# A recurrent layer on one Trainium2 core: three planes and a reduce in place of an interleaved scan, and GpSimd in place of a transfer

## The chip, the cores and the metric

The kernel runs on one core of a Trainium2 chip. The core has TensorE (PE) for matmuls, VectorE (DVE), ScalarE (ACT), GpSimd (POOL) and SyncE (SP, transfers), each with its own queue of instructions; they meet only at semaphores. The metric is the device time of the whole program in microseconds. Lower is better. A measurement of this kernel can tell apart about 0.2%, some 17 us.

## The reference

The program computes two layers of a model on x [16, 128, 128] (N = 16 rows, T = 128 steps, D = 128 channels). Each layer has a recurrent or conditioning part, a state space or attention part, a gated recurrence and a feed-forward part. Only the first of these parts is touched, a plain recurrence:

```
xw = einsum('ntd,dh->nth', x, Wx) + b
def step(prev_h, xw_t):
    next_h = tanh(prev_h @ Wh + xw_t)
    return (next_h, next_h)
_, hs = lax.scan(step, h0, swapaxes(xw, 0, 1))
```

The weights are scaled so that the recurrence magnifies small differences. The kernel therefore forms each dot product as the reference's arithmetic does: 128 products, each added in order to a running sum and rounded after each, with the product itself not rounded before the addition.

## The kernel before

The work of this layer is in the function `rnn`. A dot product over k = 0..127 is built in four moves, for all 16 n at once, with the output channels on the 128 partitions.

1. TensorE forms all 16 x 128 products in PSUM, from three bf16 pieces of each operand, with a diagonal matrix as the moving operand (`product`, `h_product`).
2. ScalarE copies them to `pd`; VectorE forms the running sums `s`: a scan for the odd ones (`prefix_odd`, L560, two halves of the n), an addition for the even ones (`prefix_even`, L564).
3. The rounding errors of the running sums are found exactly. VectorE forms the difference s - pd for the hidden half (`difference`, L567, into `gain`). TensorE adds, in PSUM, minus the sums, the difference and the products once more (`remainder`, L295, L300, L303); what is left is the remainder of every step of the sum.
4. A chain adds, for each k, minus the difference, the remainder and the sum to one running number. For this ScalarE writes the three into an interleaved layout `at` (`put_sums`, `put_differences`, `put_remainders`, L391, L394, L397, L400), and VectorE runs a scan that takes two numbers per element (`chain`, L571, four quarters of the n).

All this is done twice. The hidden half (R, prev_h @ Wh) lies on the recurrence. The input half (X, x_t @ Wx) does not depend on h and runs AHEAD = 9 steps in front: nine rounds of a prologue, and then one round beside each of the 128 steps. Its difference comes another way: ScalarE makes a negated copy `nd` of the products (`copy_negative`, L385), and a transfer from the queue of GpSimd adds the sums to it (L477, `accum_op=ALU.add`), with a small instruction ahead of it (L476).

A step runs as follows. VectorE makes h by a rational function (`tanh`, L155 to L238) and cuts it into three bf16 pieces (`pieces`). TensorE makes the hidden product (L278), ScalarE copies it in two halves (L431), and VectorE makes odd and even prefix sums and the difference. While TensorE makes the remainders (L300, L303), a correction for rounding ties (`sticky`, L311, on signs from L436 and L442) and ScalarE puts them (L400), VectorE does the input half: half of the odd scans, the even sums, four chains and their sum with the bias (`xwt`, L589). Then come four hidden chains, `pre` (L621) and tanh. In `tanh`, ScalarE makes three copies (L453 to L455) that the scan L203 waits for.

The queue of TensorE is written out by hand. After the sticky matmuls come the input half's minus sums (L295), differences (L300) and products (L303), then the next input product (L270), then a wait until ScalarE has put the input remainders (`e.wait_ge(xa, 5 * g + 5)`), then 28 filler matmuls (`stay_warm`, L327), in seven lots that wait for places in tanh (`IN_TANH`; the last lot of three waits for h), and then the hidden product of the next step. In every eighth step (s = 7) a transpose (L330) stands before the fillers; in two of eight steps GpSimd also copies stationary operands (L499, L503).

Of the kernel before, what the change touches and what calls it, by code (L numbers as in the profile page):

```python
# [28 lines left out]
BF16 = mybir.dt.bfloat16  # L29
N = 16  # L30
# [5 lines left out]
TANH_SMALL = 0.0004  # L36
# [14 lines left out]
LX = 1 + 3 * NP  # L51


def rnn(nc, ident, hs, w):
    with ExitStack() as ctx:
# [15 lines left out]
        def side(tag):  # L71
            f = dict(pd=sb(tag + "pd", [128, N, K2]), s=sb(tag + "s", [128, N, K2]), d=sb(tag + "d", [128, 2, N * LX + 1]))
            f["at"] = f["d"][:, :, 1:].rearrange("p c (n l) -> p n c l", l=LX)
            return f
        R, X = side("rh_"), side("rx_")
        R.update(part=sb("rh_part", [128, 3, N, 2], BF16), rest=sb("rh_rest", [128, 2, N]),
                 diag=sb("rh_diag", [128, 3, N, KB], BF16), gain=sb("rh_gain", [128, N, D]),
                 sg=sb("rh_sg", [128, 2, NB, 512], BF16))
        X["nd"] = sb("rx_nd", [128, N, K2])
        co = sb("co", [128, N * LX])  # L80
        ends = co[:].rearrange("p (n l) -> p n l", l=LX)[:, :, LX - 1]
        xt = co[:, 0:T * N]
# [3 lines left out]
        pre = sb("pre", [128, N]); cl = sb("cl", [128, N]); x2 = sb("x2", [128, N]); ab = sb("neg", [128, N])  # L86
        mask = sb("mask", [128, N]); big = sb("big", [128, N]); small = sb("small", [128, N])
# [4 lines left out]
        spare = R["gain"][:].rearrange("p n k -> p (n k)")  # L92
# [5 lines left out]
        rc = sb("rc", [128, N]); nn = sb("nn", [128, N]); qq = sb("qq", [128, N]); rcb = sb("rcb", [128, N])  # L98
        hi = sb("hi", [128, N]); lw = sb("lw", [128, N]); dsp = sb("dsp", [128, 2, N]); qsel = sb("qsel", [128, N])
# [5 lines left out]
        xp_mm, xl_mm, xa, xs, xd, xc, xn, xg = (sem(x) for x in ("xp_mm", "xl_mm", "xa", "xs", "xd", "xc", "xn", "xg"))  # L105
# [3 lines left out]
        A_COPIED, A_ODD, A_SEEDED, A_SIGNED, A_PUT = 2, 3, 5, 6, 8  # L109
        KA = A_PUT + 2 * NRC + 1  # L110
        V_ODD, V_EVEN, V_DIFF = 2, 3, 4
        VSUM = V_DIFF + NRC + 1
        VGUESS = VSUM + 8
        KV = VSUM + 44
# [3 lines left out]
        VSETUP = 60  # L118
# [34 lines left out]
        def tanh(tl, e, dep, tripled):  # L153
            tl.wait(dep)
            i = tl.inc(e.tensor_scalar(cl[:], pre[:], -TANH_CLAMP, TANH_CLAMP, ALU.max, ALU.min))  # L155
            n_ = tl.inc(e.tensor_scalar(ab[:], pre[:], -1.0, None, ALU.mult))
            tl.wait(i)
            i = tl.inc(e.tensor_tensor(x2[:], cl[:], cl[:], ALU.mult))
            tl.wait(n_)
# [3 lines left out]
            tl.wait(j)  # L163
            tl.inc(e.tensor_scalar(big[:], mask[:], TANH_SMALL, None, ALU.is_ge))
            tl.inc(e.scalar_tensor_tensor(out=small[:], in0=mask[:], scalar=TANH_SMALL, in1=cl[:], op0=ALU.is_lt, op1=ALU.mult))
# [43 lines left out]
            b_ = tl.inc(e.reciprocal(rc[:], den))  # L209
            a_ = tl.inc(e.tensor_tensor(nn[:], cl[:], num, ALU.mult))  # L210
            i = tl.inc(e.tensor_tensor(raw(dsp[:, 0, :]), raw(den), cut[:, 0:N], ALU.bitwise_and))
            tl.wait(a_)
            q_ = tl.inc(e.tensor_tensor(qq[:], nn[:], rc[:], ALU.mult))
# [3 lines left out]
            i = tl.inc(e.tensor_tensor(raw(hi[:]), raw(qq[:]), cut[:, 0:N], ALU.bitwise_and))  # L217
            p_ = tl.inc(e.tensor_tensor(tq[:, :, 0], qq[:], den, ALU.mult))
            tl.inc(e.tensor_tensor(rcb[:], rc[:], big[:], ALU.mult))
            tl.wait(i)  # L220
            f_ = tl.inc(e.tensor_tensor(lw[:], qq[:], hi[:], ALU.subtract))
# [5 lines left out]
            i = tl.inc(e.tensor_tensor(qsel[:], qq[:], big[:], ALU.mult))  # L227
# [3 lines left out]
            tl.wait(i)  # L231
            tl.inc(e.tensor_tensor(qsel[:], qsel[:], small[:], ALU.add))
            tl.wait(s_)
            r_ = tl.inc(e.tensor_tensor(rm[:], rm[:], tn2[:, :, 4], ALU.subtract))
            tl.wait(r_)
            r_ = tl.inc(e.tensor_tensor(rr[:], rm[:], rcb[:], ALU.mult))
            tl.wait(r_)
            return tl.inc(e.tensor_tensor(h[:], qsel[:], rr[:], ALU.add))  # L238

        def remainder_slots(F, n, odd):  # L240
            dst = F["at"][:, n, 0, 3::3] if odd else F["at"][:, n, 1, 0:LX - 1:3]
            return dst.rearrange("p n (b k) -> p n b k", b=NB)

        def remainder_sums(bank0, n, odd):
            return ps[:, bank0:bank0 + NB, :].rearrange("p b (n k c) -> p n b k c", n=N, c=2)[:, n, :, :, odd]
# [13 lines left out]
        IN_TANH = ((9, 4), (14, 4), (19, 4), (23, 4), (26, 5), (36, 4), (44, 3))  # L259
# [6 lines left out]
        def _(e):  # L266
# [25 lines left out]
            def remainder(bank0, F, stat, mov, prefixed, differenced, diff, last, own=NB, seeded=None):  # L292
                e.wait_ge(*prefixed)
                for b in range(own):
                    e.matmul(ps[:, bank0 + b, :], negid[:], piece(F, "s", b), start=True, stop=False)  # L295
                e.wait_ge(*differenced)
                for b in range(NB):
                    if b == own:
                        e.wait_ge(*seeded)
                    e.matmul(ps[:, bank0 + b, :], ident[:], diff(b), start=False, stop=False, skip_group_check=(b >= own))  # L300
# [47 lines left out]
            with e.Fori(0, T // UN // TURNS) as turn:  # L348
                for i, s in ((TURNS * turn + r, s) for r in range(TURNS) for s in range(UN)):
# [13 lines left out]
                    if s == UN - 1:  # L363
                        e.wait_ge(stl, i + 3)
                    remainder(0, X, xl_stat, x_mov((s + 1) % UN), (xs, 3 * g + 3), (xd, 16 * (g + 1)), x_diff, True).then_inc(xl_mm, 1)
                    if s == UN - 2:
                        e.wait_ge(stp, i + 3)
# [11 lines left out]
        def _(e):  # L379
# [35 lines left out]
            for g in range(AHEAD):  # L415
                if g:
                    e.wait_ge(xc, KXC * g)
# [1330 lines left out]
```

## Time and profile before

| what | value |
|---|---|
| median of 3 runs | 8299.39 us (8298.24 to 8300.0) |
| span of the profiled execution | 8311.2 us |
| recurrent layer, first h to last h | 319.0 to 4998.9 us |
| PE busy | 6754.2 us (81%) |
| DVE busy | 6987.2 us (84%) |
| ACT busy | 4891.1 us (59%) |
| POOL busy | 1902.8 us (23%) |

The profile is of one execution. Its time is its span; no other time of the same execution is at hand. A row of a timeline gives the start and the duration in us, the engine, the line, the operation and its tiles, the number of instructions merged (xN), and in brackets the idle time of the engine before it with what ended it. Shares of busy time are averages over stages with different limits; the order of starts within one step says more.

### The profile page before, as it was taken

To read this page: it belongs to the slowest core of one execution; us is meant where nothing else is said; L and a number is where in the kernel's file an instruction comes from. 1 tells how busy PE (TensorE), PEld (TensorE's weight loads), DVE (VectorE), ACT (ScalarE), POOL (GpSimd) and SP (SyncE) were. 2 spreads that over 40 slices of the span, in tenths; PEclk is the share of its full clock that TensorE was granted. 3 is DMA by queue.
4 is the path that set the end of the run, shared out by engine and by line. 5 is a ranking of instruction groups with operands and counts; after the bars stand their busy time and mean duration, and the time that the engine had idled before them with its cause. 6 is when DMAs were issued, how large, how long until landed. Compare 5 with 4: busy or idle time off the path is not lost. (4 is left out here: it accounts for less than half of the span.)

```text
span 8311.2 us, 122846 instructions
## 1 busy us (share of the span) xinstructions
PE 6754.2 (81%) x38193; PEld 2748.6 (33%) x38193; DVE 6987.2 (84%) x12707; ACT 4891.1 (59%) x5846; POOL 1902.8 (23%) x1514
## 2 busy tenths in 40 slices
PE   4788888888888888888888883588888888782889
PEld 1233333333333333333333331233333333341553
DVE  4799999999999999999999996899999999446333
ACT  3677777777777777777777772244444444222322
POOL 0000001001001001001000110588788888000000
PEclk8999999999999999999999996799999999996999
DMA  1211111111111111111111110000000000000000
GB/s 37 37 27 32 32 27 32 32 27 32 27 32 32 27 32 30 29 32 28 31 32 27 32 32 24 18 4 3 4 3 3 4 3 3 2 6 3 3 15 5
DMA packets 51335, 174.59 MB, mean 21 GB/s; under 512 B 5857, under 2 KB 13794, under 8 KB 49698
## 3 DMA queue, kind: packets, MB, share of 16 engines
q0 software_dynamic: 37264, 145.91, 9.9%
q1 hardware_dynamic: 13586, 22.47, 1.0%
q8 instruction: 273, 4.47, 0.2%
q14 instruction: 212, 1.74, 0.1%
HBM read 15.12 MB, written 7.34 MB: 3 GB/s over the span
## 5 line engine op out<-in xcount | busy, mean ns | idle before, releaser
L980 POOL TENSOR_TENSOR hc<-hh,cg 128x512 f32<-128x512 f32 x1024 | 1290.4, 1267 | 349.8 <-DVE hh L962 349.5
L902 ACT ACTIVATE ps_m<-ps_m,aneg 128x508 f32<-128x508 f32 x1024 | 674.4, 659 | 1121.2 <-DVE hh L962 1011.2
L962 DVE TENSOR_TENSOR_SCAN hh<-ps_m,bx 128x512 f32<-128x512 f32 x1024 | 1228.7, 1213 | 13.7 <-POOL bx L984 13.7
L476 POOL TENSOR_TENSOR r_gate<-ident 128x1 f32<-128x1 f32 x137 | 213.7, 1560 | 4475.4 <-DVE rx_s L564 4413.3
L327 PE MATMUL r_ps<-wdiag,whq 128*128 128x512 bf16 x4480 | 1057.7, 382 | 216.3 <-DVE rh_gain L189 76.4
L866 PE MATMUL ps_m<-hc,pick 128*128 128x512 f32 x2048 | 1056.9, 600 | 8.0 <-POOL hc L980 6.8
L571 DVE TENSOR_TENSOR_SCAN co<-rx_d 128x772 f32<-128x772 f32 x544 | 924.0, 1761 | 0.0
L571 DVE TENSOR_TENSOR_SCAN co<-rh_d 128x772 f32<-128x772 f32 x512 | 862.5, 1747 | 15.6
L300 PE MATMUL r_ps<-rx_nd,ident 128*128 128x512 f32 x1096 | 557.4, 655 | 200.7 <-DMA rx_nd<-rx_s 200.7
L327 PEld LDWEIGHTS r_ps<-wdiag,whq 128*128 128x128 bf16 x4480 | 395.3, 98 | 836.9 <-issue 139.3
L941 DVE TENSOR_TENSOR bx<-ps_m,bg 128x512 f32<-128x512 f32 x896 | 596.8, 672 | 89.4 <-PE ps_m L882 89.0
L877 PE MATMUL ps_m<-rows,ones 128*128 128x512 bf16 x1024 | 403.2, 394 | 266.0 <-ACT ps_m L902 261.7
L400 ACT ACTIVATE rx_d<-r_ps 128x1024 f32<-128x1024 f32 x274 | 406.4, 1568 | 306.1 <-PE r_ps L303 306.1
L394 ACT ACTIVATE rh_d<-rh_s 128x1024 f32<-128x1024 f32 x256 | 419.7, 1639 | 195.3 <-DVE rh_s L560 195.3
L300 PE MATMUL r_ps<-rh_gain,ident 128*128 128x512 f32 x1024 | 473.7, 605 | 42.5 <-DVE rh_gain L567 42.3
L295 PE MATMUL r_ps<-rx_s,negid 128*128 128x512 f32 x1096 | 498.4, 597 | 3.0 <-POOL xsl L503 3.0
L560 DVE TENSOR_TENSOR_SCAN rx_s<-rx_pd 128x520 f32<-128x520 f32 x274 | 337.3, 1234 | 179.2 <-ACT rx_pd L381 151.7
L391 ACT ACTIVATE rx_d<-rx_s 128x2048 f32<-128x2048 f32 x137 | 412.4, 3010 | 72.5 <-DVE xwt L589 70.6
L431 ACT ACTIVATE rh_pd<-r_ps 128x1024 f32<-128x1024 f32 x256 | 248.2, 1022 | 341.9 <-PE r_ps L278 341.9
L400 ACT ACTIVATE rh_d<-r_ps 128x256 f32<-128x256 f32 x1024 | 380.7, 519 | 100.2 <-PE r_ps L311 100.2
L866 PEld LDWEIGHTS ps_m<-hc,pick 128*128 128x128 f32 x2048 | 391.8, 192 | 131.2 <-POOL hc L980 27.9
L877 PEld LDWEIGHTS ps_m<-rows,ones 128*128 128x128 bf16 x1024 | 98.4, 96 | 1008.3 <-ACT ps_m L902 993.1
(412 smaller groups left out, 11921.0 us busy)
## 6 DMA issues: line engine op xcount, KB each, us to landing
rx_nd<-rx_s POOLq DMA_DIRECT2D x137, 1040.0 KB, 8.0
rows_scratch<-pc SPq DMA_DIRECT2D x48, 128.0 KB
rows<-rows_scratch SPq DMA_DIRECT2D x128, 48.0 KB
ew<-in_e SPq DMA_DIRECT2D x3, 1024.0 KB, 7.4
co<-in_x_dn SPq DMA_DIRECT2D x1, 1024.0 KB, 4.8
xcur<-in_x_dn SPq DMA_DIRECT2D x1, 1024.0 KB
out_x<-xcur SPq DMA_DIRECT2D x1, 1024.0 KB, 3.9
qi<-in_f_q SPq DMA_DIRECT2D x1, 384.0 KB, 3.0
```

What stands on the lines that cost most here:

```text
L295: e.matmul(ps[:, bank0 + b, :], negid[:], piece(F, "s", b), start=True, stop=False)
L300: e.matmul(ps[:, bank0 + b, :], ident[:], diff(b), start=False, stop=False, skip_group_check=(b >= own))
L327: e.matmul(ps[:, bank, :], whq[:, 0, :], wdiag[:, 0, 0:N, :].rearrange("p m k -> p (m k)"), start=True, stop=True)
L394: e.activation(F["at"][:, :, c, 2::3], F["s"][:, :, 2 + c:K2:2], ACT.Copy).then_inc(done, 1)
L400: e.activation(remainder_slots(F, n, odd), remainder_sums(bank0, n, odd), ACT.Copy).then_inc(done, 1)
L571: return e.tensor_tensor_scan(co[:, at], F["d"][:, 0, 1:][:, at], F["d"][:, 1, 0:N * LX][:, at], 0.0, ALU.add, ALU.add)
L866: e.matmul(ps[:, 6, :], pick[:, 128 - un:256 - un], hc[un % NHC][:], start=False, stop=True, skip_group_check=True).then_inc(summed, 1)
L877: e.matmul(ps[:, un % 2, :], ones3[:], rows[0][b][:, j, :], start=True, stop=True).then_inc(dt_bc, 1)
L902: e.activation(da[un % NDA][:, :, 1:T], ps[:, un % 2, :].rearrange("p (n t) -> p n t", n=NG4)[:, :, 1:T], ACT.Exp, scale=aneg[:, 0:1]).the ...
L941: e.tensor_tensor(bx[un % NBUF][:], ps[:, 2 + un % 2, :], bg[:], ALU.mult).then_inc(driven, 1)
L962: e.tensor_tensor_scan(hh[un % NBUF][:], da[un % NDA].rearrange("p n t -> p (n t)"), bx[un % NBUF][:], 0.0, ALU.mult, ALU.add).then_inc(sc ...
L980: e.tensor_tensor(hc[un % NHC][:], hh[un % NBUF][:], cg[:], ALU.mult).then_inc(weighted, 1)
```

## The change

The interleaved layout goes. Each half gets three planes, `planes` [128, 3, N, K2], holding minus the difference (pd - s), the remainder and the sum; `s`, `nd` and `rho` are views of them. The chain becomes a `tensor_reduce` over k and, inside it, the plane, for a quarter of the n, so ScalarE only copies remainders (one put per quarter for the hidden half, two for the input half) and no longer copies sums and differences. The input half's even prefix sums and difference are made by GpSimd; the transfer and the negated copy go. In TensorE's queue the input half's minus sums are followed by the next input product, and only then by the differences and products of the remainder. On VectorE the first quarter of the input chain moves ahead of the hidden prefix sums, the other three ahead of both odd scans of the input half. In tanh, the masks and the arithmetic select are replaced by one comparison of the square and a predicated copy. The diff, cut to its core:

```diff
+            f = dict(pd=sb(tag + "pd", [128, N, K2]), planes=sb(tag + "planes", [128, 3, N, K2]), ends=sb(tag + "ends", [128, N]))
+            f["nd"], f["rho"], f["s"] = (f["planes"][:, c] for c in (MINUS_D, RHO, SUM))
...
 def tanh
-            n_ = tl.inc(e.tensor_scalar(ab[:], pre[:], -1.0, None, ALU.mult))
-            j = tl.inc(e.tensor_tensor(mask[:], ab[:], pre[:], ALU.max))
-            tl.inc(e.tensor_scalar(big[:], mask[:], TANH_SMALL, None, ALU.is_ge))
-            tl.inc(e.scalar_tensor_tensor(out=small[:], in0=mask[:], scalar=TANH_SMALL, in1=cl[:], op0=ALU.is_lt, op1=ALU.mult))
+            tl.inc(e.tensor_scalar(small[:], x2[:], TANH_SMALL_SQUARED, None, ALU.is_lt))
...
-            tl.inc(e.tensor_tensor(rcb[:], rc[:], big[:], ALU.mult))
-            i = tl.inc(e.tensor_tensor(qsel[:], qq[:], big[:], ALU.mult))
-            tl.inc(e.tensor_tensor(qsel[:], qsel[:], small[:], ALU.add))
+            tl.inc(e.copy_predicated(quot[:], raw(small[:]).unsqueeze(1).to_broadcast([128, 2, N]), plain[:]))
+            tl.wait(s_ + 1)
...
-        IN_TANH = ((9, 4), (14, 4), (19, 4), (23, 4), (26, 5), (36, 4), (44, 3))
+        IN_TANH = ((6, 4), (11, 4), (16, 4), (20, 4), (23, 5), (32, 4), (39, 3))
...
 tensor, in each step
                     sticky(4, (ra, KA * t + A_SIGNED))
+                    minus_sums(0, X, (xs, 3 * g + 3))
+                    if s == UN - 2:
+                        e.wait_ge(stp, i + 3)
+                    e.wait_ge(ra, KA * t + A_SIGNED + NRC)
+                    product(4, xp_stat, x_mov((s + 2) % UN)).then_inc(xp_mm, 1)
                     if s == UN - 1:
                         e.wait_ge(stl, i + 3)
-                    remainder(0, X, xl_stat, x_mov((s + 1) % UN), (xs, 3 * g + 3), (xd, 16 * (g + 1)), x_diff, True).then_inc(xl_mm, 1)
-                    e.wait_ge(ra, KA * t + A_PUT + 2 * NRC)
-                    product(4, xp_stat, x_mov((s + 2) % UN)).then_inc(xp_mm, 1)
-                    e.wait_ge(xa, 5 * g + 5)
+                    remainder(0, X, xl_stat, x_mov((s + 1) % UN), (xd, g + 1), True).then_inc(xl_mm, 1)
+                    e.wait_ge(xa, KXA * g + 3)
...
 scalar, in each step
-                    put_sums_of(R, 1, ra)
-                    put_sums_of(R, 0, ra)
-                    put_differences(R, R["gain"][:], ra)
                     for c in range(NRC):
-                        for odd in range(2):
-                            put_remainders(R, 4, quarter(c), odd, ra)
-                    e.wait_ge(xc, KXC * g)
-                    parts(g, 0)
+                        put_remainders(R, 4, quarter(c), ra)
                     (the three copies t1, t1, t0)
+                    x_remainders(g)
+                    x_products(g + 1)
-                    copy_out(X, 4, xa)
-                    copy_negative(xn)
...
 gpsimd
             def x_difference(g):
+                e.wait_ge(xc, KXC * g)
+                e.wait_ge(xs, 3 * g + 2)
+                e.tensor_tensor(X["s"][:, :, 2:K2:2], X["s"][:, :, 1:D:2], X["pd"][:, :, 2:K2:2], ALU.add).then_inc(xs, 1)
                 e.wait_ge(xs, 3 * g + 3)
-                e.tensor_tensor(gate[:, 2:3], ident[:, 0:1], ident[:, 1:2], ALU.add).then_inc(xg, 1)
-                e.dma_start(flat(X["nd"][:]), flat(X["s"][:]), accum_op=ALU.add, max_dma_last_dim=4 * N * K2 // 2).then_inc(xd, 16)
+                e.tensor_tensor(X["nd"][:, :, 2:K2], X["pd"][:, :, 2:K2], X["s"][:, :, 2:K2], ALU.subtract).then_inc(xd, 1)
...
 vector
+            def chain(F, n):
+                return e.tensor_reduce(F["ends"][:, n], F["planes"][:, :, n, 2:K2].rearrange("p c n k -> p n k c"), XY, ALU.add)
...
-                    x_prefix_odd(g, HALVES[0])
+                    x_chain_first(g - 1)
                     (hidden odd and even prefix sums, difference)
-                    x_prefix_odd(g, HALVES[1])
-                    x_prefix_even(g)
-                    x_chain(g - 1, s)
+                    x_chain_rest(g - 1, s)
+                    x_prefix(g)
                     (four hidden chains, pre, tanh, pieces)
```

## Rows read from the trace of the kernel before

**Rows 1.** The line that writes h: starts over all steps; duration min/median/max in ns.

```profile
L238 DVE TENSOR_TENSOR h<-qsel,rr x128: 174/174/178, 319.0 to 4998.9; 128x16 f32<-128x16 f32 x128
```

**Rows 2.** Timeline of VectorE in one ordinary step.

```profile
2417.01 0.17 DVE L238 TENSOR_TENSOR h<-qsel,rr 128x16 f32<-128x16 f32 x1
...
2420.72 2.37 DVE L560 TENSOR_TENSOR_SCAN rh_s<-rh_pd 128x520 f32<-128x520 f32 x2 [0.41 <-ACT rh_pd L431]
...
2426.60 1.24 DVE L560 TENSOR_TENSOR_SCAN rx_s<-rx_pd 128x520 f32<-128x520 f32 x1
...
2429.01 6.73 DVE L571 TENSOR_TENSOR_SCAN co<-rx_d 128x772 f32<-128x772 f32 x4
...
2436.08 6.74 DVE L571 TENSOR_TENSOR_SCAN co<-rh_d 128x772 f32<-128x772 f32 x4
2442.85 0.18 DVE L621 TENSOR_TENSOR pre<-co,xwT 128x16 f32<-128x16 f32 x1
...
2453.13 0.18 DVE L238 TENSOR_TENSOR h<-qsel,rr 128x16 f32<-128x16 f32 x1
```

**Rows 3.** Timeline of TensorE in the same step.

```profile
2432.42 1.90 PE L311 MATMUL r_ps<-rh_sg,r_tau 128*128 128x512 bf16 x8
2434.16 3.60 PE L295 MATMUL r_ps<-rx_s,negid 128*128 128x512 f32 x8
2438.74 3.70 PE L300 MATMUL r_ps<-rx_nd,ident 128*128 128x512 f32 x8 [0.98 <-DMA rx_nd<-rx_s]
2442.38 2.12 PE L303 MATMUL r_ps<-wdiag,xsl 32*128 32x512 bf16 x36
2444.33 1.46 PE L270 MATMUL r_ps<-wdiag,xsp 32*128 32x512 bf16 x24
2447.65 6.54 PE L327 MATMUL r_ps<-wdiag,whq 128*128 128x512 bf16 x28 [1.85 <-DVE rh_gain L189]
2454.14 1.60 PE L278 MATMUL r_ps<-rh_diag,whq 32*128 32x512 bf16 x24
```

**Rows 4.** Timeline of ScalarE in the same step.

```profile
2419.66 1.94 ACT L431 ACTIVATE rh_pd<-r_ps 128x1024 f32<-128x1024 f32 x2 [2.14 <-PE r_ps L278]
...
2434.36 2.97 ACT L400 ACTIVATE rh_d<-r_ps 128x256 f32<-128x256 f32 x8 [0.80 <-PE r_ps L311]
...
2444.55 2.97 ACT L400 ACTIVATE rx_d<-r_ps 128x1024 f32<-128x1024 f32 x2 [1.52 <-PE r_ps L303]
```

**Rows 5.** VectorE's groups by line and form: busy us, mean ns, idle before.

```profile
L138 DVE TENSOR_TENSOR rh_part<-rh_rest,nought 128x32 bf16<-128x32 f32 x258 | 47.6, 184 | 0.0
...
L225 DVE TENSOR_TENSOR tq<-lw,dsp 128x32 f32<-128x32 f32 x128 | 25.1, 196 | 0.0
...
L1340 DVE TENSOR_REDUCE fmu<-fyc 128x16 f32<-128x2048 f32 x3 | 6.9, 2286 | 0.1
...
L1516 DVE TENSOR_REDUCE amu<-aoa 128x256 f32<-128x2048 f32 x1 | 3.6, 3566 | 0.0
...
L1495 DVE TENSOR_REDUCE aaq<-ae 128x256 f32<-128x1024 f32 x1 | 1.2, 1220 | 0.0
```

**Rows 6.** Two lines of GpSimd: duration min/median/max in ns.

```profile
L980 POOL TENSOR_TENSOR hc<-hh,cg x1024: 1260/1266/1447, 5272.8 to 7064.9; 128x512 f32<-128x512 f32 x171
...
L476 POOL TENSOR_TENSOR r_gate<-ident x137: 193/1572/1582, 49.5 to 4974.9; 128x1 f32<-128x1 f32 x137
```

**Rows 7.** Timeline of TensorE in a step whose transfer landed late.

```profile
2549.21 5.40 PE L300 MATMUL r_ps<-rx_nd,ident 128*128 128x512 f32 x8 [2.35 <-DMA rx_nd<-rx_s]
...
2559.78 6.21 PE L327 MATMUL r_ps<-wdiag,whq 128*128 128x512 bf16 x28 [1.83 <-ACT rx_d L400]
```

**Rows 8.** Windows: busy time of each engine, granted clock (PEclk), DMA share, GB/s.

```profile
2549.00:2552.00 3.00, 2.79 (x4) 1.26 (x5) 2.97 (x3) 3.00 (x2) 0.00 (x0) 0.58 0.00 0
```

**Rows 9.** VectorE's waits between 400 and 4900 us: total us, times, longest.

```profile
DVE rh_s L560 <- ACT rh_pd L431: 86.8, 122, 2.5
DVE to L203 <- ACT t L455: 36.4, 24, 2.0
```

More of the change, by code:

```diff
@@ L50 @@
 TURNS = 2
-LX = 1 + 3 * NP
+MINUS_D, RHO, SUM = 0, 1, 2
+XY = mybir.AxisListType.XY
 def rnn(nc, ident, hs, w):
@@ L290, in residue, with minus_sums @@
                 return ins
-            def remainder(bank0, F, stat, mov, prefixed, differenced, diff, last, own=NB, seeded=None):
+            def minus_sums(bank0, F, prefixed, own=NB):
                 e.wait_ge(*prefixed)
@@ L295, in remainder @@
                     e.matmul(ps[:, bank0 + b, :], negid[:], piece(F, "s", b), start=True, stop=False)
+            def remainder(bank0, F, stat, mov, differenced, last, own=NB, seeded=None):
                 e.wait_ge(*differenced)
@@ L564, in prefix_even @@
                 return e.tensor_tensor(F["s"][:, :, 2:K2:2], F["s"][:, :, 1:D:2], F["pd"][:, :, 2:K2:2], ALU.add)
-            def difference(out, F):
-                return e.tensor_tensor(out, F["s"][:, :, 2:K2], F["pd"][:, :, 2:K2], ALU.subtract)
-            def chain(F, lo, hi_):
-                at = slice(lo * LX, hi_ * LX)
-                return e.tensor_tensor_scan(co[:, at], F["d"][:, 0, 1:][:, at], F["d"][:, 1, 0:N * LX][:, at], 0.0, ALU.add, ALU.add)
-            def x_prefix_odd(g, part, later=True):
-                e.wait_ge(xa, 5 * g + 1)
-                if later:
-                    e.wait_ge(xd, 16 * g)
-                prefix_odd(X, part).then_inc(xs, 1)
@@ new lines, in chain, with x_prefix, x_chain_first, x_chain_rest @@
+            def chain(F, n):
+                return e.tensor_reduce(F["ends"][:, n], F["planes"][:, :, n, 2:K2].rearrange("p c n k -> p n k c"), XY, ALU.add)
+            def x_prefix(g):
+                e.wait_ge(xa, KXA * g + 1)
+                for part in HALVES:
+                    prefix_odd(X, part).then_inc(xs, 1)
+            def x_chain_first(g):
+                e.wait_ge(xa, KXA * g + 2)
+                chain(X, quarter(0)).then_inc(xc, 1)
+            def x_chain_rest(g, u):
+                tx = Tally(e, xc, KXC * g + 1)
+                e.wait_ge(xa, KXA * g + 3)
+                for c in range(1, NXC):
+                    tx.inc(chain(X, quarter(c)))
@@ L588, in x_chain @@
                 tx.wait(tx.n)
-                tx.inc(e.tensor_tensor(xwt[:, N * u:N * (u + 1)], ends, brow[:, N * u:N * (u + 1)], ALU.add))
+                tx.inc(e.tensor_tensor(xwt[:, N * u:N * (u + 1)], X["ends"][:], brow[:, N * u:N * (u + 1)], ALU.add))
             for g in range(AHEAD):
-                for part in HALVES:
-                    x_prefix_odd(g, part, g > 0)
-                x_prefix_even(g)
                 if g:
-                    x_chain(g - 1, g - 1)
+                    x_chain_first(g - 1)
+                    x_chain_rest(g - 1, g - 1)
@@ L609, in _ @@
                     tl.wait(j)
[L610 to L614 removed]
+                    tl.inc(difference(R))
+                    x_chain_rest(g - 1, s)
+                    x_prefix(g)
                     for c in range(NRC):
[L616 to L617 removed]
+                        e.wait_ge(ra, KA * t + A_SIGNED + c + 1)
+                        j = tl.inc(chain(R, quarter(c)))
                     tl.wait(j)
@@ L620, in _ @@
                         e.wait_ge(xw_cp, i + 1)
-                    j = tl.inc(e.tensor_tensor(pre[:], ends, xwT[:, s, :], ALU.add))
+                    j = tl.inc(e.tensor_tensor(pre[:], R["ends"][:], xwT[:, s, :], ALU.add))
                     j = tanh(tl, e, j, (tri, 3 * t + 3))
```

160 lines of the change are left out of this document (53 added, 107 removed).

## The prediction

> **What bounds the kernel now.** I read the page first: VectorE and TensorE are both busy for over four fifths of the span, so shares alone do not say which decides. Then the 128 steps of the recurrent layer, by the starts of the instruction that writes h: 319.0 to 4998.9 us over 127 steps, 36.85 us each [rows 1]. The change touches nothing behind them. The timelines of one ordinary step say what sets its length [rows 2 to 4]. The reader is to see a ring. VectorE's rows stand nearly back to back from the hidden half's prefix sums (2420.72) to h (2453.13); the only hole is 0.41 us before the prefix sums, waiting for ScalarE's copy of the new product. TensorE runs the input half's work from 2434.16 to 2445.79, with a hole of 0.98 us for the transfer, waits for ScalarE's puts, and starts the 28 filler matmuls at 2447.65. They end at 2454.19, and the next hidden product starts at 2454.14. The last three fillers wait for h, so VectorE decides, but TensorE arrives only just in time. I count all times below from D = 2426.60, the start of VectorE's first row behind the hidden difference. In these terms: hidden chains start at 9.48, `pre` at 16.25, fillers at 21.05, next hidden product 27.54 to 29.14.
>
> **The prices first.** *Reduce.* A quarter goes from a scan over 772 pairs (four take 6.74, thus 1.66 from start to start [rows 2]) to a reduce over 4x128x3 = 1536 numbers. Reduces over 2048 and 1024 contiguous numbers take 2286 and 1220 ns, so 1.04 ns a number and 154 fixed; one over 2048 whose inner step is 64 bytes takes 3566 ns, 1.67 a number [rows 5]. Then 1536 numbers cost 1.75 us at full rate and 2.71 us at the strided rate; 0.08 less from start to start. The new reduce takes each number from another plane, 8320 bytes off, and returns to the first plane's neighbour after three. No row shows that pattern. The nearest in form is L225: its second input alternates between two rows 64 bytes apart and takes 196 ns for 32 elements, against 184 for L138 and some 20 ns more that the strided rate would add [rows 5]; so an alternation of two lines seems free, a round of eight (L1516) is not, and three lies between. I take the full rate, and keep the strided one as a rival.
>
> The Trainium skill speaks against this step. "Advanced Engine Details and Errata", section Memory Cachelines, says that accesses which each hit another 16-byte line are penalised; by it every reduce would pay the strided rate. "Vector Engine (DVE) Microarchitecture Reference", section Measured stream behaviour on trn2, gives 1.73 ns for a source that hops with every element, but full rate for one stream alternating between two regions. The rows above bear out both, and neither page has three planes. By the first rule the time would be that of rival B below, 9010 us; by the second, carried over to three planes, my sum.
>
> *GpSimd.* A two-input operation over 512 numbers takes 1260 ns at least, and one over a single number 193 ns when alone [rows 6]: 2.09 ns a number. The even prefix sums (1024) are then 2.33 us and the difference (2048) 4.47 us. Bounds for the first: 1.23, what VectorE takes for it, and 2.52, twice the row. The row with 1572 ns for one number stands beside a VectorE scan with two inputs in SBUF: the engines can block each other. In the new order VectorE runs reduces (one input) while GpSimd works, and GpSimd's 1260 ns row holds beside VectorE work with only one SBUF input; I take no blocking.
>
> *ScalarE.* It loses the copies of sums and differences into the interleaved layout and the negated copy. That is worth only what waits for it: VectorE's wait before L203, 36.4 us in all [rows 9]. A put of a quarter is now one row of 512 numbers, about 0.6 us, between the old puts of 256 (eight in 2.97) and copies of 1024 (two in 1.94) [rows 4].
>
> *Tanh.* Seven small rows go, two come. They mostly filled gaps that a dependency leaves anyway (cl to x2 to xm start 0.21 apart with or without them). The predicated copy has no row; between 0.11 and 0.25 us as other small ones, and the subtraction now waits for it. Net -0.05, bounds -0.3 and +0.2.
>
> **A step of the new kernel, from D.** VectorE: three input chains 5.07 us, the sum into xwt and two odd prefix scans (1.15 + 1.23) end at 7.6. The hidden chains wait for the first put: the sticky matmuls end at 7.72 as before, ScalarE puts 0.6, start 8.4 in place of 9.48. Four chains bring `pre` to 15.15, 1.1 earlier, and h to 25.4. The input chain moved before the hidden prefix sums takes 1.66 where a scan of 1.23 with 0.41 of waiting stood: nothing lost beyond 0.1.
>
> TensorE is now late instead. Its first input matmuls need the even prefix sums, which VectorE had ready long before and GpSimd delivers at 7.65 + 2.33, so they start at 10.05 in place of 7.56. Everything queued behind them in order follows: eight f32 matmuls with the sums 3.64 (as from 2438.74 to 2442.38 [rows 3]), the next input product 1.30 (24 of the 36 from 2442.38 to 2444.33), the difference matmuls 3.64 and the 36 remainder matmuls, 2.17 to ScalarE's start: 20.8. GpSimd's difference is done by 14.6, under the product, and costs nothing. ScalarE's two puts are one pair of 1024 from PSUM, 1.94 [rows 4]: 22.75. The fillers wait for these puts and start at 22.9 in place of 21.05, although h now comes earlier. Twenty-eight of them cannot be skipped: in the step of 2559.78, where they did not wait for h, they still took 6.2 us [rows 7]. The hidden product so starts at 29.05 and, all its inputs ready, takes 1.46 as the input product of the same size: it ends at 30.5 in place of 29.14. From there ScalarE's copy, the prefix sums and the difference follow as before. **Plus 1.4 us a step**; VectorE's gain of 1.1 turns into waiting for the hidden product.
>
> Two corrections. In 30 of the 125 steps between 330 and 4990 us the transfer into rx_nd lands late and TensorE stands 2.2 to 2.4 us (the row of 2549.21 is one); I take each as 0.9 us longer, since an ordinary step takes 36.12 (h at 2417.01 and 2453.13 [rows 2]) and the mean is 36.85, of which the loop's own turns leave about a third to them. With no transfer that ends: -27 us. But in 18 of these 30 TensorE then ran its f32 matmuls at a lower granted clock (0.58 over 2549 to 2552, 5.40 us in place of 3.70 [rows 7, 8]); after the 95 shorter gaps never. The new order makes a gap of 2.3 us (7.72 to 10.05) in every step. With 18 in 30: 0.6 x 1.7 = 1.0 us, now on the path: +131 us. The prologue (nine rounds without the hidden half, before 319.0) swaps the 8 us transfer for GpSimd's 6.9 and loses two memsets, but puts a chain before each prefix scan; nothing, within 30. GpSimd's copies for xsp and xsl now stand ahead of its two operations, but fall in the previous tanh, where VectorE has slack. Sum: 128 x 1.4 = 179, -27, +131 = **+283 us**, on 8299.39: **8582 us**, say 8580. The profiled execution spans 8311.2, 12 us over the median of the runs; I carry that over.
>
> **The rivals.** *B, the reduce pays the strided rate* (for it: L1516; against it: L225). Input chains end at 7.97, prefix scans at 10.5, hidden chains take 10.6: `pre` at 21.1, 4.85 later, and the chain moved ahead delays the prefix sums by 2.63 - 1.64 = 1.0. TensorE then has slack, bar the clock. 5.85 x 128 = 749, less some 40 for the late steps: about 9010, up to 9080 with the low clock.
>
> *F, TensorE keeps up* (the other side). If fillers end before h, VectorE's sum holds: -1.1 + 0.1 - 0.05 = -1.05 a step, 134 us, and the waits for ScalarE beyond the usual 0.41, (86.8 - 122 x 0.41) + 36.4 = 73 us [rows 9]: 8092. It decides only where the input puts are done by `pre` + 4.9; my sum has them at `pre` + 7.6. For it: the fillers before took no longer than h allowed, and my prices for GpSimd and for the puts are borrowed from other shapes; against it: they would have to be wrong by 2.7 us together. *S, GpSimd is as quick as VectorE* (1.23 for the even sums): 1.1 us less, +0.3 a step, the clock gap gone: 8299 + 38 - 27, within 0.2%. *C, the reduce pays part* (1.2 to 1.5 ns a number): 8650 to 8900.
>
> **How the numbers follow.** A (the forecast) 0.48, own range 8430 without the clock loss to 8660 with it every step. B 0.29, C 0.05, F 0.13, S 0.05. Faster by over 0.2% (about what a measurement of this kernel can tell from no change) is F, the same is S, slower is the rest: 0.13, 0.05, 0.82. The range leaves out F, S and a tip of B: 8400 to 9060.
>
> **What would show it.** Right: TensorE's first input matmuls wait about 2.3 us for GpSimd; the fillers start later than `pre` + 7 and run without holes; VectorE waits some 3 us before the hidden prefix sums, released by ScalarE's copy; the reduce of 1536 numbers takes 1.75 us; the difference matmuls show a granted clock below 1 in more than half of the steps. Wrong: reduces of 2.7 us and no wait before the prefix sums (B), or fillers that still wait for h (F). GpSimd's rows would also show a blocking that I left out: an even sum far over 2.33 us.

## The result and the profile after

| | before | after |
|---|---|---|
| median | 8299.15 us (4 runs, 8298.24 to 8300.0) | 8830.35 us (4 runs, 8824.28 to 8831.31) |
| ratio | 1 | 1.064, 95% interval 1.0627 to 1.0653 |
| span of the profiled execution | 8311.2 us | 8829.3 us |
| mean granted clock of TensorE in it | 0.950 | 0.925 |

Slower by 531 us. The time lies in the stated range (8400 to 9060) and 250 us above the predicted 8580; it is also above the forecast's own range, 8430 to 8660.

First the line that writes h, from its source view; columns as in [rows 1].

```profile
L229 DVE TENSOR_TENSOR h<-quot,rr x128: 174/175/177, 303.6 to 5515.8; 128x16 f32<-128x16 f32 x128
```

The recurrence takes 41.04 us a step where it took 36.85 [rows 1]: 127 x 4.19 = 532 us. It begins 15 us earlier; the prologue no longer has the 8 us transfers, but what made these 15 us was not tested apart. Together that is 517 of the 518 us between the spans.

Now an ordinary step, on the timelines of VectorE, TensorE, ScalarE and GpSimd, beside [rows 2 to 4]. The prediction's time zero, D, is 2616.30 here.

```profile
2610.43 2.37 DVE L510 TENSOR_TENSOR_SCAN rh_planes<-rh_pd 128x520 f32<-128x520 f32 x2 [4.44 <-ACT rh_pd L397]
...
2616.30 5.55 DVE L520 TENSOR_REDUCE rx_ends<-rx_planes 128x4 f32<-128x1536 f32 x3
...
2622.01 2.37 DVE L510 TENSOR_TENSOR_SCAN rx_planes<-rx_pd 128x520 f32<-128x520 f32 x2
2624.70 7.39 DVE L520 TENSOR_REDUCE rh_ends<-rh_planes 128x4 f32<-128x1536 f32 x4 [0.31 <-ACT rh_planes L369]
2632.13 0.18 DVE L566 TENSOR_TENSOR pre<-rh_ends,xwT 128x16 f32<-128x16 f32 x1
...
2642.23 0.18 DVE L229 TENSOR_TENSOR h<-quot,rr 128x16 f32<-128x16 f32 x1
```

```profile
2622.13 1.90 PE L297 MATMUL r_ps<-rh_sg,r_tau 128*128 128x512 bf16 x8
2627.33 5.40 PE L279 MATMUL r_ps<-rx_planes,negid 128*128 128x512 f32 x8 [3.30 <-POOL rx_planes L430]
2632.66 1.47 PE L254 MATMUL r_ps<-wdiag,xsp 32*128 32x512 bf16 x24
2634.07 3.70 PE L286 MATMUL r_ps<-rx_planes,negid 128*128 128x512 f32 x8
2637.70 2.12 PE L289 MATMUL r_ps<-wdiag,xsl 32*128 32x512 bf16 x36
2642.00 6.21 PE L311 MATMUL r_ps<-wdiag,whq 128*128 128x512 bf16 x28 [2.18 <-DVE rm L225]
2648.15 1.47 PE L262 MATMUL r_ps<-rh_diag,whq 32*128 32x512 bf16 x24
```

```profile
2639.93 1.94 ACT L369 ACTIVATE rx_planes<-r_ps 128x1024 f32<-128x1024 f32 x2 [5.27 <-PE r_ps L289]
```

```profile
2624.46 2.81 POOL L430 TENSOR_TENSOR rx_planes<-rx_planes,rx_pd 128x1024 f32<-128x1024 f32 x1 [32.71 <-DVE rx_planes L510]
2627.36 4.55 POOL L432 TENSOR_TENSOR rx_planes<-rx_pd,rx_planes 128x2048 f32<-128x2048 f32 x1
```

These rows show that the ring has changed hands: TensorE, no longer VectorE, sets when the next step can begin. VectorE has a hole of 4.44 us ahead of the hidden prefix sums (before 0.41 [rows 2]). TensorE stands 3.30 us for GpSimd's even prefix sums, runs the first eight f32 matmuls in 5.40 us instead of 3.60 [rows 3], and starts the fillers at D + 25.70 instead of 21.05. h is written at 2642.23, the fillers end at 2648.2, and the hidden product of the next step follows at 2648.15. The profile names a row of tanh behind the fillers' wait of 2.18 us (DVE L225), the event next before it; their first lot waits for a much earlier place in tanh and for ScalarE's puts, and these end at 2641.87: they held TensorE.

VectorE's waits between 400 and 5300 us say the same of all steps, beside [rows 9]:

```profile
DVE rh_planes L510 <- ACT rh_pd L397: 608.2, 119, 6.5
DVE rh_ends L520 <- ACT rh_planes L369: 40.7, 120, 1.0
```

And two windows show the granted clock, columns as in [rows 8]: 0.66 over the eight matmuls behind the hole (a stretch with both levels, 1.2 and 2.4 GHz, in it), 1.00 (2.4 GHz) over hidden matmuls of the same kind.

```profile
2616.00:2620.00 4.00, 3.66 (x9) 1.43 (x8) 4.00 (x4) 2.12 (x2) 0.00 (x0) 1.00 0.00 0
2627.00:2632.00 5.00, 4.67 (x7) 2.03 (x8) 5.00 (x3) 0.00 (x0) 4.83 (x2) 0.66 0.00 0
```

Read in windows of 300 us between 400 and 5500 us, the timeline has 122 whole groups of these eight (one that a window's edge divides is not counted, here and in the counts below); 119 take 5.1 to 5.4 us, three take 3.7. The fillers are hit too: of 123 whole lots, 48 take 7.7 to 7.9 us and 75 take 6.2. Before, all 124 took 6.2 to 6.7.

### The profile page after: what moved, and what is told of

It reads as the page before. It is cut to its first block and busy times, and to the rows that moved or that the text cites. A ratio compares the mean times of both kernels' runs of the same rounds, so it can differ in the third digit from the quotient of the medians.

```text
span 8829.3 us, 119213 instructions
## 1 busy us (share of the span) xinstructions
PE 7005.5 (79%) x38193; PEld 2831.6 (32%) x38193; DVE 6968.0 (79%) x11925; ACT 2872.1 (33%) x4538; POOL 2484.4 (28%) x1513
## 5 line engine op out<-in xcount | busy, mean ns | idle before, releaser
L430 POOL TENSOR_TENSOR rx_planes<-rx_planes,rx_pd 128x1024 f32<-128x1024 f32 x137 | 385.2, 2812 | 4254.8 <-DVE rx_planes L510 4254.8
L520 DVE TENSOR_REDUCE rx_ends<-rx_planes 128x4 f32<-128x1536 f32 x544 | 1013.7, 1906 | 151.2 <-ACT rx_planes L369 132.6
L279 PE MATMUL r_ps<-rx_planes,negid 128*128 128x512 f32 x1096 | 739.2, 838 | 481.9 <-POOL rx_planes L430 481.9
L520 DVE TENSOR_REDUCE rh_ends<-rh_planes 128x4 f32<-128x1536 f32 x512 | 946.3, 1911 | 43.2 <-ACT rh_planes L369 43.2
L510 DVE TENSOR_TENSOR_SCAN rh_planes<-rh_pd 128x520 f32<-128x520 f32 x256 | 303.8, 1228 | 655.0 <-ACT rh_pd L397 655.0
L432 POOL TENSOR_TENSOR rx_planes<-rx_pd,rx_planes 128x2048 f32<-128x2048 f32 x137 | 622.6, 4545 | 10.7
L279 PEld LDWEIGHTS r_ps<-rx_planes,negid 128*128 128x128 f32 x1096 | 278.8, 265 | 895.2 <-POOL rx_planes L430 544.7
L369 ACT ACTIVATE rx_planes<-r_ps 128x1024 f32<-128x1024 f32 x274 | 265.7, 1022 | 856.9 <-PE r_ps L289 856.9
L369 ACT ACTIVATE rh_planes<-r_ps 128x512 f32<-128x512 f32 x512 | 264.4, 604 | 755.3 <-PE r_ps L297 755.3
L286 PE MATMUL r_ps<-rh_planes,negid 128*128 128x512 f32 x1024 | 473.2, 605 | 42.0 <-DVE rh_planes L517 42.0
L286 PE MATMUL r_ps<-rx_planes,negid 128*128 128x512 f32 x1096 | 506.1, 604 | 0.0
```

The source lines that it names most:

```text
L286: e.matmul(ps[:, bank0 + b, :], negid[:], piece(F, "nd", b), start=False, stop=False, skip_group_check=(b >= own))
L369: e.activation(F["rho"][:, n, 2:K2].rearrange("p n (b k) -> p n b k", k=KB), ps[:, bank0:bank0 + NB, :].rearrange("p b (n k) -> p n b k", ...
L432: e.tensor_tensor(X["nd"][:, :, 2:K2], X["pd"][:, :, 2:K2], X["s"][:, :, 2:K2], ALU.subtract).then_inc(xd, 1)
L520: return e.tensor_reduce(F["ends"][:, n], F["planes"][:, :, n, 2:K2].rearrange("p c n k -> p n k c"), XY, ALU.add)
```

## The experiments

Each edit is made on the kernel after the change unless another is named. "Before" ran beside them on the same chip, with medians of 8304.21 (1 to 4), 8300.98 (5 to 8) and 8300.53 us (9 to 11) in the three sets; a difference taken across sets can be off by the 5 us in which these differ.

**1. Half the fillers.** Is TensorE's queue what sets the step?

```diff
-        IN_TANH = ((6, 4), (11, 4), (16, 4), (20, 4), (23, 5), (32, 4), (39, 3))
+        IN_TANH = ((6, 2), (11, 2), (16, 2), (20, 2), (23, 2), (32, 2), (39, 2))
```

> The changed kernel with 14 filler matmuls a step in place of 28. Theory (TensorE's queue sets the step: late input work, then fillers that no longer wait for h): the fillers take 3.1 us less, the next hidden product starts 3.1 us earlier and VectorE's wait before the hidden prefix sums falls from 4.5 to 1.4 us: 128 x 3.1 = 397 us less, about 8433 us. Rival 1 (VectorE or ScalarE decides and the fillers only fill): no change, 8830. Rival 2 (the fillers hold the clock up): the lower count costs granted clock in the matmuls behind them, and part of the gain is lost, 8500 to 8900.

Measured: 8416.36 us (ratio to before 1.0136, interval 1.0119 to 1.0153), 414 less than after. VectorE's wait before the hidden prefix sums falls from 608 us in 119 steps to 228 us in 124. So the queue of TensorE is the bound, and 3.1 us less of it gives 3.2 us a step. All 122 groups of the input sums still take 5.1 us or more, behind the same hole.

**2. The even prefix sums on VectorE again.** Is it GpSimd's time, and the hole it makes?

```diff
 vector, x_prefix
+                e.wait_ge(xs, 3 * g + 2)
+                prefix_even(X).then_inc(xs, 1)
 gpsimd, x_difference
-                e.wait_ge(xs, 3 * g + 2)
-                e.tensor_tensor(X["s"][:, :, 2:K2:2], X["s"][:, :, 1:D:2], X["pd"][:, :, 2:K2:2], ALU.add).then_inc(xs, 1)
```

> The changed kernel with the input half's even prefix sums made by VectorE again, behind its odd scans; the difference stays on GpSimd. Theory: TensorE's first input matmuls start 1.6 us earlier (VectorE takes 1.23 us where GpSimd takes 2.81), the gap before them falls from 3.3 to 1.7 us, the granted clock does not fall and the eight matmuls take 3.70 in place of 5.40: 3.3 us a step less, 8830 - 422 = 8408 us. VectorE's own row is longer by 1.2 us a step and is paid from its wait. Rival (only the start counts, the clock falls for another reason): 1.6 us a step, 8625. Rival (VectorE decides): 1.2 us a step more, 8980.

Measured: 8406.05 us (1.0124, interval 1.0107 to 1.0141), 424 less than after, where 422 were expected. The TensorE row of a step:

```profile
2616.78 3.70 PE L279 MATMUL r_ps<-rx_planes,negid 128*128 128x512 f32 x8 [1.67 <-DVE rx_planes L512]
```

The hole is 1.67 us and the clock holds: 111 groups behind such a hole, all at 3.7 us. This one row given to GpSimd is four fifths of the whole loss. VectorE's 1.23 us more are paid out of its wait.

**3. Fillers in the hole.** Is it the standing that lowers the clock?

```diff
                     sticky(4, (ra, KA * t + A_SIGNED))
+                    stay_warm(1, 12)
                     minus_sums(0, X, (xs, 3 * g + 3))
```

> The changed kernel with 12 more filler matmuls (2.7 us) between the sticky matmuls and the input half's minus sums, where TensorE otherwise stands for 3.3 us. Theory (the standing is what lowers the granted clock): the eight f32 matmuls behind it take 3.70 us in place of 5.40, although they start at the same time: 1.7 us a step less, 8830 - 218 = 8612 us. Rival (5.40 us is the price of these operands while GpSimd or VectorE works, not the clock): the rows stay at 5.40 and the time at 8830 or a little above.

Measured: 8670.28 us (1.0442, interval 1.0425 to 1.046), 160 less than after.

```profile
2632.96 2.75 PE L311 MATMUL r_ps<-wdiag,whq 128*128 128x512 bf16 x12
2636.45 3.70 PE L279 MATMUL r_ps<-rx_planes,negid 128*128 128x512 f32 x8 [0.73 <-POOL rx_planes L431]
```

All 123 groups behind the shorter hole take 3.7 us, at the same start; so it is the standing, not the operands or GpSimd beside them. The 58 us that are missing went to the other wait: 76 of 121 lots of the 28 fillers now run slow, not 48 of 123. At 1.7 us each that is 0.24 x 1.7 x 128 = 52 us.

**4. Contiguous addresses.** Are 1.91 and 2.81 us prices of the pattern? The kernel sums in another order and makes other even sums, as the expectation says.

```diff
-                e.tensor_tensor(X["s"][:, :, 2:K2:2], X["s"][:, :, 1:D:2], X["pd"][:, :, 2:K2:2], ALU.add).then_inc(xs, 1)
+                e.tensor_tensor(X["s"][:, :, 2:2 + D // 2], X["s"][:, :, 2 + D // 2:K2], X["pd"][:, :, 2:2 + D // 2], ALU.add).then_inc(xs, 1)
...
-                return e.tensor_reduce(F["ends"][:, n], F["planes"][:, :, n, 2:K2].rearrange("p c n k -> p n k c"), XY, ALU.add)
+                return e.tensor_reduce(F["ends"][:, n], F["planes"][:, :, n, 2:K2].rearrange("p c n k -> p n c k"), XY, ALU.add)
```

> The changed kernel where the reduce reads the same three planes in another order, k innermost and contiguous, then the plane (so it sums in another order), and where GpSimd's even prefix sums read and write 64 contiguous numbers of each row in place of every second one (so those sums are others). Everything else stays. Theory (the two misjudged prices are the price of the address pattern): the reduce falls from 1.91 to 1.75 us, GpSimd's row from 2.81 to 2.33, TensorE's gap from 3.3 to about 2.3 us; 1.0 us a step less if the clock still falls (8702), 2.7 less if it no longer does (8485). Rival (1.91 and 2.81 are what so many numbers cost in any order): rows and time stay as they are, 8830.

Measured: 8616.65 us (1.0392, interval 1.0367 to 1.0417), 214 less than after. The groups by form (busy us, mean ns):

```profile
L521 DVE TENSOR_REDUCE rx_ends<-rx_planes 128x4 f32<-128x1536 f32 x476 | 810.6, 1744 | 18.5 <-issue 18.5
...
L430 POOL TENSOR_TENSOR rx_planes<-rx_planes,rx_pd 128x1024 f32<-128x1024 f32 x119 | 281.9, 2369 | 3717.1 <-DVE rx_planes L511 3717.1
```

and on the page of the kernel after the change:

```profile
L430 POOL TENSOR_TENSOR rx_planes<-rx_planes,rx_pd 128x1024 f32<-128x1024 f32 x137 | 385.2, 2812 | 4254.8 <-DVE rx_planes L510 4254.8
...
L520 DVE TENSOR_REDUCE rx_ends<-rx_planes 128x4 f32<-128x1536 f32 x544 | 1013.7, 1906 | 151.2 <-ACT rx_planes L369 132.6
```

The prediction's 1.75 and 2.33 us were the contiguous prices, to 0.04 us. Three planes cost the reduce 0.16 us more, every second number costs GpSimd 0.44. The hole shrinks to 2.38 us, and the clock falls in 61 of 120 steps. That accounts for the time: 128 x (3 x 0.16 + 0.44) = 118 us for the prices and 128 x 0.47 x 1.7 = 102 for the clock make 220; against it, 60 of 124 lots of fillers run slow, where 48 of 123 did (20 us). The sum is 200 for the 214 measured.

**5. Tanh alone**, on the kernel before:

```diff
+            tl.inc(e.tensor_scalar(small[:], x2[:], TANH_SMALL_SQUARED, None, ALU.is_lt))
...
+            tl.inc(e.copy_predicated(quot[:], raw(small[:]).unsqueeze(1).to_broadcast([128, 2, N]), plain[:]))
```

> The kernel before with only the new tanh (one comparison of the square and a predicated copy); the two halves, the transfer and the interleaved scan stay as they were. From pre to h VectorE's rows take 10.28 us in the trace before (2442.85 to 2453.13) and 10.10 in the trace after (2632.13 to 2642.23). Theory (VectorE decides in the kernel before, so what tanh saves shows in full): 128 x 0.18 = 23 us less, about 8281. Rival (TensorE is only just in time, so the fillers cap the gain) or the 0.05 us a step of the prediction: 0 to 7 us less, 8297 to 8304.

Measured: 8292.42 us (11 runs; ratio 0.9991, interval 0.9982 to 1.0), 9 us less. The predicated copy takes 0.17 us. The 23 us of the first theory are outside the interval, up to 15 us inside; the predicted 6 us are inside, and so is no change at all. This part explains none of the 531 us.

**6. Two sets of planes.** If the hole comes from VectorE reaching the input prefix sums only behind the three input chains, they can go first, once the sums of one step don't overwrite what the chains of the last one read.

```diff
+        X2 = dict(X, planes=sb("ry_planes", [128, 3, N, K2]))
+        SIDES = (X, X2)
 gpsimd and scalar: side (s + 1) % 2, and
-                e.wait_ge(xc, KXC * g)
+                e.wait_ge(xc, KXC * (g - 1))
 vector, behind the hidden difference
-                    x_chain_rest(g - 1, s)
-                    x_prefix(g)
+                    x_prefix(g, (s + 1) % 2)
+                    x_chain_rest(g - 1, s, s % 2)
```

> The changed kernel with two sets of input planes that alternate by step, so that GpSimd and ScalarE no longer wait for the input chain of the step before; VectorE makes the input half's odd prefix sums first, behind the hidden difference, and then the three input chains. Theory: GpSimd's even prefix sums are ready 5.3 us behind the hidden difference instead of 11.0, before TensorE is through with the sticky matmuls; the gap of 3.3 us and the low clock behind it go. The input phase from 7.7: sums 3.64, product 1.4, differences and remainder 5.8, puts 2.1, fillers at 20.7, next hidden product at 26.9 where before had 27.54: 0.6 us a step under before, 27 for the late transfers, 15 for the prologue. With the low clock behind the 2.2 us wait for the puts, as in 48 of 123 steps of the changed kernel (1.7 us each, 80 us): 8304 - 119 + 80 = 8265 us. Rival (GpSimd beside VectorE's reduces slows, or the input chains delay the hidden ones): VectorE's hidden chains start over 1 us later, 8400 or more.

Measured: 8474.59 us (1.0211, interval 1.0198 to 1.0225), 210 over the expectation and in the range of its rival. The hole ahead of the input sums is gone as expected, but the hidden chains start 9.86 us behind the hidden difference, where they started at 8.40. The timelines of VectorE, GpSimd, ScalarE and TensorE show two things that the theory had not:

```profile
2611.68 5.54 DVE L526 TENSOR_REDUCE rx_ends<-ry_planes 128x4 f32<-128x1536 f32 x3
2617.25 2.07 DVE L543 TENSOR_TENSOR xwt<-rx_ends,r_brow 128x16 f32<-128x16 f32 x1
2619.25 7.37 DVE L526 TENSOR_REDUCE rh_ends<-rh_planes 128x4 f32<-128x1536 f32 x4
```

```profile
2614.75 4.55 POOL L438 TENSOR_TENSOR rx_planes<-rx_pd,rx_planes 128x2048 f32<-128x2048 f32 x1
```

```profile
2628.76 0.41 ACT L416 ACTIVATE t<-xm 128x176 f32<-128x176 f32 x1
2629.01 1.91 ACT L372 ACTIVATE rx_planes<-r_ps 128x1024 f32<-128x1024 f32 x2
```

```profile
2625.52 2.12 PE L292 MATMUL r_ps<-wdiag,xsl 32*128 32x512 bf16 x36
2631.45 7.18 PE L314 MATMUL r_ps<-wdiag,whq 128*128 128x512 bf16 x27 [3.80 <-DVE r_spare L186]
```

A sum of 16 numbers takes 2.07 us and ends at 2619.32, when GpSimd's difference ends (2619.30); the reduces beside the same row take what they take alone. The Trainium skill says so in general ("SBUF — State Buffer", section SBUF: two separate sides): a VectorE instruction with two inputs in SBUF and one of GpSimd that reads SBUF share a pair of ports as a lock, and whoever comes second waits for the other's end. The trace agrees, within 0.02 us. And the input puts wait on ScalarE behind the three copies for tanh, so TensorE, done with the remainder at 2627.6, stands: 3.80 us by the row, which has 27 of the 28 fillers, and at least the 3.3 us until the puts end at 2630.92. Nearly all lots of fillers run slow (122 of 124 take 7.3 us or more for 28, or at that rate).

**7. The old order of TensorE too.** On the kernel of 6, remainder first and then the next input product.

```diff
-                    e.wait_ge(ra, KA * t + A_SIGNED + NRC)
-                    product(4, xp_stat, x_mov((s + 2) % UN)).then_inc(xp_mm, 1)
                     remainder(0, SIDES[(s + 1) % 2], xl_stat, x_mov((s + 1) % UN), (xd, g + 1), True).then_inc(xl_mm, 1)
+                    e.wait_ge(ra, KA * t + A_SIGNED + NRC)
+                    product(4, xp_stat, x_mov((s + 2) % UN)).then_inc(xp_mm, 1)
```

> As the kernel with two sets of planes, and TensorE's order as before the change: minus sums, differences and remainder, and only then the next input product. Theory: the product now covers 1.4 us of ScalarE's puts, so TensorE waits under 1.5 us for them and the fillers keep the clock: fillers at about 20.1, about 0.5 us a step under the kernel above and none of its 80 us: 8190 us. Rival (the fillers are held by VectorE's places in tanh, so it gains only the clock): 8190 to 8250. Rival (the difference from GpSimd is late for the new order, over 11.4 us): a new gap before the difference matmuls, no gain over the kernel above.

Measured: 8490.51 us (1.0233, interval 1.0219 to 1.0247): 16 us more than 6, where 8190 was expected. In the step read TensorE is through at 2630.66 and its row of 27 fillers begins 4.42 us later, behind puts that end at 2634.56 since they again stand behind the three copies. The order is not what held it; ScalarE's queue is, which 10 tests.

**8. Fewer fillers**, on the kernel of 7: 3, 3, 3, 3, 3, 3 and 2 instead of 28 in all.

> As the kernel with two sets of planes and the old order, with 20 fillers in place of 28 (1.8 us less). Theory (with the gap gone the step is set by VectorE again, and TensorE is at most 0.5 us late): 0 to 60 us less than the kernel above. Rival (the fillers still set the step): 1.8 us a step, 230 us less. Rival (fewer fillers cost clock): slower than the kernel above.

Measured: 8398.55 us (1.0117, interval 1.0102 to 1.0133), 92 less than 7, which none of the three had: under the 230 of the fillers' full price, over the 60 of the theory. The fillers still lie on the path (eight of them at full clock are 1.8 us a step), but the low clock persists: 19 take 6.99 us in the step read, where 27 took 7.18 in the kernel of 6. That this is why the gain is under 230 was not tested apart.

**9. The sum with the bias moved**, on the kernel of 7, behind the hidden chains.

```diff
-                    x_chain_rest(g - 1, s, s % 2)
+                    tx = x_chain_rest(g - 1, s, s % 2)
...
                         j = tl.inc(chain(R, quarter(c)))
+                    x_sum(tx, s)
```

> As the kernel with two sets of planes and the old order, and one row moved: VectorE's sum of the input chains with the bias (16 numbers, two inputs in SBUF) stands behind the four hidden chains instead of ahead of them. In the kernels with two sets of planes it takes 2.07 us in place of 0.17 and ends when GpSimd's difference ends. Theory (VectorE's row with two inputs waits for GpSimd's row with two inputs, its reduces do not): moved, it takes 0.17 again, the hidden chains start 1.5 us earlier, and so do pre and h; TensorE's wait ahead of the fillers falls from 4.4 to about 2.9 us or less. At least 1.5 us a step less, 8490 - 192 = 8298 us, and down to 8200 if the clock of the fillers comes back. Rival (the 2 us are a wait for something else): the row stays at 2 us in its new place, and the time at 8490.

Measured: 8241.16 us (0.9935, interval 0.9919 to 0.9952), 249 less than 7, within what was expected (192 less, and more if the clock comes back). It did in part: 75 of 125 lots of fillers still run slow, where all did in 7. The sum's row, duration min/median/max, in the kernel of 6 and in this one:

```profile
L543 DVE TENSOR_TENSOR xwt<-rx_ends,r_brow x136: 174/2074/2143, 66.0 to 5141.6; 128x16 f32<-128x16 f32 x136
```

```profile
L546 DVE TENSOR_TENSOR xwt<-rx_ends,r_brow x136: 158/166/176, 65.7 to 4918.5; 128x16 f32<-128x16 f32 x136
```

**10. The puts first.** On the kernel of 9, ScalarE's input puts ahead of the copies for tanh.

```diff
+                    x_remainders(g, (s + 1) % 2)
                     e.wait_ge(v, KV * t + V0 + VGUESS)
...
                     e.activation(t0[:, :, 0], line(xm), ACT.Copy).then_inc(tri, 1)
-                    x_remainders(g, (s + 1) % 2)
```

> As the kernel with the sum moved, and ScalarE makes the two puts of the input remainders ahead of its three copies for tanh instead of behind them. Theory (TensorE is through with the remainder 16.8 us behind the hidden difference, while the copies wait for a row of tanh at about 17.4 and hold the puts back): TensorE waits at most 0.5 us ahead of the fillers, the clock stays up, and VectorE sets the step: h at 25.9 where the kernel before has 26.53. 0.63 x 128 = 81 us, 27 for the late transfers and 15 for the prologue under the kernel before: 8180 us. Rival (TensorE stays the later one, or the late puts make tanh wait for the copies): no better than the kernel with the sum moved.

Measured: 8181.24 us (0.9859, interval 0.9842 to 0.9875), 119 under before, one microsecond off the expectation. TensorE and ScalarE:

```profile
2631.18 1.46 PE L257 MATMUL r_ps<-wdiag,xsp 32*128 32x512 bf16 x24
2633.53 3.73 PE L314 MATMUL r_ps<-wdiag,whq 128*128 128x512 bf16 x16 [0.88 <-DVE r_spare L176]
```

```profile
2631.46 1.94 ACT L372 ACTIVATE rx_planes<-r_ps 128x1024 f32<-128x1024 f32 x2 [6.93 <-PE r_ps L292]
```

The puts start as the remainder ends, TensorE waits 0.88 us, and the fillers run at full clock and wait for VectorE again; from 400 to 4900 us the granted clock is 0.99, where it was 0.95 in 7.

**11. 24 fillers**, on the kernel of 10.

> As the kernel with the puts first, and 24 fillers in place of 28. Theory (VectorE sets the step now): within 20 us of the kernel with the puts first. Rival (the fillers still set it): 0.9 us a step, 115 us less. Rival (clock): more.

Measured: 8183.64 us (0.9866, interval 0.9849 to 0.9882), the same as 10: 0.9 us less of fillers a step gives nothing. TensorE's queue no longer sets the step, and VectorE's rows do.

## Why the prediction was right or wrong

*What bounds the kernel before: it fits.* By the rows VectorE decides, with TensorE only just in time. In that kernel itself only 5 changed VectorE alone, by too little to tell, so this rests on the rows. The kernel after the change moved as TensorE's queue said, with less work on TensorE (1) and with more on VectorE (2).

*The ring of the new kernel: right.* TensorE late through GpSimd's even sums, fillers that do not wait for h, VectorE's gain turned into a wait before the hidden prefix sums. Step by step, in us from D:

| | predicted | measured |
|---|---|---|
| odd scans end | 7.6 | 8.08 |
| first hidden chain | 8.4 | 8.40 |
| input sums on TensorE start | 10.05 | 11.03 |
| `pre` | 15.15 | 15.83 |
| first input put | 20.8 | 23.63 |
| fillers start | 22.9 | 25.70 |
| next hidden product starts | 29.05 | 31.85 |

The 2.80 us between the last two are: three reduces of 1.91 us for 1.75, 0.48 up to the scans' end; GpSimd's 2.81 for 2.33, 0.48; the low clock, 1.69, which the prediction carried apart as 1.0; and 0.15 of small change.

*The reduce: mis-sized.* "I take the full rate" gave 1.75 us; it is 1.91, four in 7.39. Rival B (2.71 us) is excluded. The reading of L225 as free was loose: its 12 ns over L138 are more than half of the 20 that the strided rate would add. The Trainium skill's rule on 16-byte lines ("Advanced Engine Details and Errata", Memory Cachelines) penalises every such read and names no rate. The trace agrees that there is a penalty, 0.16 us in 1536 numbers (4), a tenth; the strided rate that the prediction put in its place, 2.71 us, is not what such reads paid. The time does lie in the range of rival C, but not by its mechanism: 1.91 us is 1.14 ns a number behind the fixed 154 ns, under its 1.2 to 1.5, and of the reduces only the three input ones lie on the path, ahead of the scans that GpSimd waits for.

*GpSimd: mis-sized.* The price came from a row with contiguous numbers; experiment 4 finds it to 0.04 us, and 0.44 more for every second number. The bound from above, 2.52, was too low, since both bounds were drawn without the pattern.

*The clock: the largest error.* "In 18 of 30" was read off holes of 2.2 to 2.4 us. The hole became 3.3 by the two prices above, and behind it the clock fell in 119 of 122 steps: 128 x 1.65 = 211 us for the predicted 131. The counts ahead of eight f32 matmuls, by the length of the stand: behind 0.7 us none of 123 (3); 1.67, none of 111, and 2.0, three of 8 (2); 2.2 to 2.4, 18 of 30 in the kernel before and 12 of 28 in that of 5; 2.4, 61 of 119 (4); 3.3, nearly all. So the misjudged half microseconds counted twice, once as time and once by what the hole then did.

*A term that was missing.* The wait ahead of the fillers grew from 1.85 [rows 3] to 2.18 us, since the input product no longer stands between the remainder and them, and in 48 of 123 steps the fillers then ran slow: 128 x 0.39 x 1.7 = 85 us. The prediction asked about the clock only at the hole it had found.

*The sum over.* 1.4 + 0.96 + 0.15 a step are 321 us, the low clock adds 211 and 85, the late transfers take 27 off and the prologue, which the prediction had at nothing within 30, takes 15: 575. The spans differ by 518 (the medians by 531, since the profiled execution of before ran 12 over its median). The 57 left are 0.45 us a step. The trace of the kernel before puts most of them in the term for the late transfers. By the starts of h, and without the seven steps in which the loop turns, the 72 steps with no late transfer in them or in the step ahead take 36.05 us on the mean, and the 46 others 37.35: 46 x 1.30 = 60 us, where the prediction has 27. It took 0.9 us for each of the 30 late steps; they take 1.4 us more, and 16 steps behind them are 1.1 us longer too. With 60 the sum is 542, and 24 us stay open.

*The range: part luck.* The ring and its waits came as forecast, but the time is above the forecast's own range. It lies in the stated one because that reaches up to 9060 for rival B, which the rows exclude.

*ScalarE and tanh: right,* close to nothing on the path (ScalarE's busy time falls from 4891 to 2872 us all the same). *Rivals F and S* are excluded by the 3.3 us hole. No blocking between GpSimd and VectorE, as predicted for this order: VectorE runs reduces there. The blocking is real, though, as soon as a row with two inputs falls beside GpSimd (6, 9).

## What to carry to other kernels

When work moves to a slower engine, ask what its consumer on a third engine did not wait for until now, and price the wait with everything queued in order behind it. Price an operation from a row with the same address pattern, and where the result makes an engine stand, work out the time at the next longer hole as well: here a hole of 1.67 us cost its length alone, and one of 3.3 us cost 1.7 us more in nearly every step, by the clock. A loss of 531 us became a gain of 119 with the same reduce and the same GpSimd work: the consumers had to be moved out of its way, a second set of buffers, one sum of 16 numbers and one pair of puts.

## What the runs showed of the hardware

- VectorE's sum of 16 numbers with two inputs in SBUF takes 0.17 us, and 2.07 us behind GpSimd's difference, ending with it; three reduces take 5.54 beside GpSimd and 5.55 without.
- A reduce of 1536 numbers takes 1.74 us with the contiguous dimension innermost and 1.91 when each number comes from another of three planes. GpSimd adds 1024 numbers in 2.37 us from contiguous rows and in 2.81 from every second place.
- TensorE's granted clock fell after it had stood, not by which matmuls came next: filling the stand with 12 matmuls kept eight f32 matmuls at 3.70 us instead of 5.40. The share of slow lots of fillers at the next wait was then 76 of 121, where it had been 48 of 123.
